# Sorted experts of a recurrent block on Trainium2: inner rows computed turned from fp16 halves, biases as a product, halves made by GpSimd in the narrow attention

## The chip, the cores and the metric

One core of one Trainium2 chip runs the whole program: four attention-like layers and four expert layers over 4096 tokens of 128 features. The metric is the device time of one execution in microseconds, the median of the runs shown. Less is better.

## The reference, cut to what matters

Three of the steps matter here. Layer 1 has an attention of 16 heads of 8 features, and then a mixture of 8 experts of which each token takes 2 (8192 rows to compute). Layer 2 has a mixture of the same shape, of which each token takes 2 too but with room for 5120 rows in all. An expert is

```
h = gelu(x @ W1[e] + b1[e])        # x 128 features, W1 128 x 512
y = h @ W2[e] + b2[e]              # W2 512 x 128
out = sum over the chosen experts of share * y
```

All inputs and outputs are fp32. The experts' biases are part of what is computed.

## The kernel before, in words

The program is a row of stages with a barrier of all engines behind each. Every engine's order of work is written out by hand; engines meet by semaphores alone.

**Narrow attention** (`narrow_attention_stage`, from L623) has 16 items of 4 heads, each with 32 steps in which TensorE computes scores (L798), row maxima of the item ahead (L784) and the weighted sum (L814), ScalarE the exponentials (L848) and VectorE the maxima (L865). Beside it GpSimd runs `RowScatter.run` (L1730): 64 indirect DMAs (L1745) that send the tokens' rows to the place where their expert's rows lie together, 4 in each item, each held back by a count of scores. SyncE loads the weights of one expert in each of items 0, 1, 3, 5, ... (`load_expert`, L1721) and clears one eighth of a table of results in items 2, 4, ... .

**Sorted experts** (`sorted_experts_stage`, from L1822) runs twice: `experts1` over 72 blocks of 128 rows (it also holds the output projection of the attention, after block 11), `experts2` over 40. A block belongs to one expert, whose number lies in a table. For a block n the engines do:

- TensorE: `turn_x` turns x of block n + 2 (L1927); `project` reads the expert's number into a register (`expert_of`, L1916) and makes rows of the inner layer in one fp32 product of 512 columns, with the tokens as the stationary operand (L1934); `turn_h` turns h of block n in four fp32 products (L1941); `down` reads the expert's number once more and sums four fp32 products (L1950).
- VectorE: `add_bias` (L2011) adds b1, kept in all 128 partitions, and `finish` (L2016) adds b2. Each reads the expert's number too.
- ScalarE: Gelu (L1990), a copy of the turned x (L1983) and of the turned h (L1996).
- GpSimd: `keep` (L1896) copies the row's target and share, `send` multiplies by the share (L1901), waits for its own result, and starts the indirect DMA of 128 rows (L1904).
- SyncE: loads x of a block ahead (L1883, L1890).

The tiles with two buffers (x turned, `up`, h, `out`) let TensorE be one block ahead of ScalarE in `project` and one behind in `down`. Most of the blocks run in a hardware loop that holds four of them; all addresses of weights are made of the expert's register at run time.

**Combine and send** (`combine_and_send_stage`, from L2530) stands between the two and loads all weights of the second experts at once (L1683 to L1685).

Of the kernel before, what the change touches and what calls it, by code (L numbers as in the profile page):

```python
# [9 lines left out]
ALU = mybir.AluOpType  # L10
# [614 lines left out]
def narrow_attention_stage(nc, ident, q_d, k_d, v_d, o_d, l_d, max_d, beside):  # L625
# [28 lines left out]
    with Stage(nc, "attn1") as st:  # L654
# [32 lines left out]
        def _(sp):  # L687
# [60 lines left out]
            body(0, 0, True, False, lambda: job.load_expert(sp, LOOPS))  # L748
            with sp.Fori(0, LOOPS) as j:
                body(2 * j + 1, 1, False, False, lambda: job.load_expert(sp, j))  # L750
                body(2 * j + 2, 0, False, False, lambda: job.clear(sp, j))
            body(NI - 1, 1, False, True, lambda: job.clear(sp, LOOPS))
# [915 lines left out]

class ExpertWeights:

    LOADS = 3

    def __init__(self, ctx, nc, name, weights_d):
        self.weights_d = weights_d
        E, _, F = weights_d[0].shape
        sb = lambda n, width: ctx.enter_context(nc.sbuf_tensor(f"{name}_{n}", [P, width], F32))
        self.w1, self.b1, self.w2 = (sb(n, E * F) for n in ("w1", "b1", "w2"))

    def load(self, sp, loaded):  # L1680

        w1_d, b1_d, w2_d, _ = self.weights_d
        sp.dma_start(self.w1[:].rearrange("d (e f) -> d e f", e=w1_d.shape[0]), w1_d.rearrange("e d f -> d e f")).then_inc(loaded, DMA)  # L1683
        sp.dma_start(self.b1[:], broadcast_rows(b1_d.rearrange("e f -> (e f)"))).then_inc(loaded, DMA)
        sp.dma_start(self.w2[:].rearrange("p (k d) -> p k d", d=D), w2_d.rearrange("e (k p) d -> p (e k) d", p=P)).then_inc(loaded, DMA)  # L1685

    def load_one(self, sp, e, loaded):

        w1_d, b1_d, w2_d, _ = self.weights_d
        F = w1_d.shape[2]  # L1690
        own = bass.ds(e * F, F)
        sp.dma_start(self.w1[:, own], w1_d[bass.ds(e, 1)].rearrange("a d f -> d (a f)")).then_inc(loaded, DMA)
        sp.dma_start(self.b1[:, own], broadcast_rows(b1_d.rearrange("e f -> (e f)")[own])).then_inc(loaded, DMA)
        sp.dma_start(self.w2[:, own].rearrange("p (k d) -> p k d", d=D),
                     w2_d[bass.ds(e, 1)].rearrange("a (k p) d -> p (a k) d", p=P)).then_inc(loaded, DMA)

class RowScatter:

    def __init__(self, st, held, send_d, share_d, xs_d, weights, blank_d=None):
        self.held, self.send_d, self.share_d, self.xs_d, self.weights, self.blank_d = held, send_d, share_d, xs_d, weights, blank_d
        self.share = st.sb("share", [P, 2, NT])
        self.send = st.sb("send", [P, 2, NT], I32)
        self.rows = st.sb("sent_rows", [P, NT, ROW])
        self.loaded, self.sent, self.weights_in = st.sem("send_loaded"), st.sem("sent"), st.sem("weights_in")
        self.copied, self.numbered = st.sem("rows_copied"), st.sem("numbered")
        if blank_d is not None:
            self.blank, self.blank_made, self.blanked = st.sb("blank", [P, BLANK * D]), st.sem("blank_made"), st.sem("blanked")
            self.experts, self.clears = weights.weights_d[0].shape[0], blank_d.shape[0] // (P * BLANK)  # L1710
# [5 lines left out]
    def load_weights(self, sp):  # L1716
        self.weights.load(sp, self.weights_in)

    def load_expert(self, sp, e):
        self.weights.load_one(sp, e, self.weights_in)  # L1720
# [9 lines left out]
    def run(self, pool, nc, hold=None):  # L1730

        if self.blank_d is not None:
            nc.gpsimd.memset(self.blank[:], 0.0).then_inc(self.blank_made, 1)
        pool.wait_ge(self.loaded, 2 * DMA)
        pool.wait_ge(self.copied, 1)
        for j in range(2):
# [11 lines left out]
        if self.blank_d is None:  # L1748
            pool.wait_ge(self.weights_in, self.weights.LOADS * DMA)
        else:  # L1750
            pool.wait_ge(self.weights_in, self.weights.LOADS * DMA * self.experts)
            pool.wait_ge(self.blanked, DMA * self.clears)
# [69 lines left out]
def sorted_experts_stage(nc, name, ident, blocks, xs_d, expert_d, weights, y_d, beside=None):  # L1822
# [4 lines left out]
    E = 8  # L1827
    F = 4 * D
    FT = F // P
    UNROLL = 4  # L1830
    NL = blocks // UNROLL
    assert blocks % UNROLL == 0 and NL >= 3
    with Stage(nc, name) as st:
        x, y = st.sb("x", [P, UNROLL, ROW]), st.sb("y", [P, blocks, D])
        result = st.sb("result", [P, blocks, 2], I32)
        w1, b1, w2 = weights.w1, weights.b1, weights.w2
        b2 = st.sb("b2", [P, E * D])
        expert = st.sb("expert", [1, blocks], I32)
        xT = st.sb("xT", [P, 2, P])
        pre, hid = st.sb("pre", [P, 2, F]), st.sb("hid", [P, 2, F])  # L1840
        hidT = st.sb("hidT", [P, 2, F])
        xt = st.ps("xt", [P, 2, CH])
        up = st.ps("up", [P, 2, F])
        ht = st.ps("ht", [P, 2, F])
        out = st.ps("out", [P, 2, CH])
        names = ("consts", "x_turned", "x_copied", "projected", "biased", "gelu_done", "h_turned", "h_copied", "summed", "y_ready")
        (consts, x_turned, x_copied, projected, biased, gelu_done, h_turned, h_copied, summed, y_ready) = (st.sem(n) for n in names)
        stored, kept, shared, loaded = st.sem("stored"), st.sem("kept"), st.sem("shared"), [st.sem(f"loaded{u}") for u in range(UNROLL)]
        job = beside(st) if beside else None
        block = st.block()  # L1850
        NCONST = 2

# [18 lines left out]
        def _(sp):  # L1871
            sp.dma_start(expert[:], expert_d[:]).then_inc(consts, DMA)
            sp.dma_start(b2[:], broadcast_rows(weights.weights_d[3].rearrange("e d -> (e d)"))).then_inc(consts, DMA)
# [19 lines left out]
        def _(pool):  # L1893
# [12 lines left out]

            for n in range(blocks + UNROLL - 1):
# [11 lines left out]
        def _(pe):  # L1919
            mm = nc.tensor.matmul  # L1920

            def turn_x(n, u, any_before):

                pe.wait_ge(loaded[u], DMA * ((n - u) // UNROLL + 1))
                if any_before:
                    pe.wait_ge(x_copied, n - 1)
# [1622 lines left out]
```

## Time and profile before

| what | us |
|---|---|
| median of 3 runs (3450.25 to 3453.23) | 3452.64 |
| profiled execution: span from first to last instruction, the only time given for it | 3455.0 |
| narrow attention, 1925 to 2567 | 642 |
| sorted experts 1, 2567 to 2798 | 231 |
| combine and send, 2798 to 2979 | 181 |
| sorted experts 2, 2979 to 3104 | 125 |

### The profile page before, as it was taken

Reading aid. Unit: us, or ns where it says so; the run is one execution under the profiler, and the core shown is the slowest. Engines: PE = TensorE matmul, PEld = TensorE weight load, DVE = VectorE, ACT = ScalarE, POOL = GpSimd, SP = SyncE. Lnnn points to the kernel's source line nnn. Section 1 sums busy time; section 2 is a strip of 40 time slices with the busy share of each in tenths; the row PEclk is TensorE's granted clock in tenths of the full one; section 3 lists DMA queues with packets and bytes.
Section 4 is the critical chain, followed back from the end, with each engine's and each line's share of the span. In section 5 each row is a group of like instructions: output and inputs, shape, how many; then the busy total and the mean of one; then the engine's idle time right before and its main releaser. Section 6 shows DMA issues by size and latency. Waiting matters only on the chain. (4 is left out here: it accounts for less than half of the span.)

```text
span 3455.0 us, 66767 instructions
## 1 busy us (share of the span) xinstructions
PE 2862.4 (83%) x21143; PEld 1283.2 (37%) x21144; DVE 2338.1 (68%) x3360; ACT 1849.0 (54%) x3005; POOL 1552.6 (45%) x1224
## 2 busy tenths in 40 slices
PE   3999999999999996799965599999978932484994
PEld 1333333333333334633323122222226622352772
DVE  5666666666666663788886799999944348534663
ACT  2555555555555551154463399999973443244442
POOL 0898999899989996200000011110115625460000
PEclk9999999999999997899986699999999965696995
DMA  2111111111111113500003222222221151113001
GB/s 86 31 42 47 43 52 46 42 48 42 56 42 48 42 48 119 197 1 1 0 2 126 66 49 56 54 53 53 53 85 47 46 182 42 29 39 100 11 13 55
DMA packets 263894, 189.55 MB, mean 55 GB/s; under 512 B 148174, under 2 KB 209990, under 8 KB 262576
## 3 DMA queue, kind: packets, MB, share of 16 engines
q1 hardware_dynamic: 255568, 174.05, 17.6%
q0 software_dynamic: 8224, 14.24, 1.3%
q8 instruction: 51, 0.84, 0.1%
q14 instruction: 51, 0.42, 0.0%
HBM read 105.21 MB, written 67.55 MB: 50 GB/s over the span
## 5 line engine op out<-in xcount | busy, mean ns | idle before, releaser
L331 POOL TENSOR_TENSOR attn_esum<-attn_esum,attn_prob 128x1024 f32<-128x1024 f32 x384 | 904.7, 2356 | 30.3 <-ACT attn_prob L482 6.7
L553 DVE TENSOR_REDUCE attn_half_max<-attn_peek 128x2 f32<-128x1024 f32 x512 | 627.0, 1225 | 398.7 <-PE attn_peek L382 394.9
L482 ACT ACTIVATE attn_prob<-attn_score 128x1024 f32<-128x1024 f32 x512 | 512.5, 1021 | 247.4 <-PE attn_score L365 247.4
L848 ACT ACTIVATE attn_prob<-attn_score 128x512 f32<-128x512 f32 x1024 | 556.3, 596 | 73.2 <-PE attn_score L798 59.0
L865 DVE TENSOR_REDUCE attn_half_max<-attn_peek 128x2 f32<-128x1024 f32 x512 | 583.5, 1214 | 11.5 <-PE attn_peek L784 11.4
L412 PE MATMUL attn_acc<-attn_prob,attn_v 128*64 128x512 f32 x2048 | 487.9, 597 | 0.1
L814 PE MATMUL attn_acc<-attn_prob,attn_v 128*32 128x256 f32 x4096 | 328.2, 392 | 12.1 <-ACT attn_out L840 10.6
L1745 POOL DMA_INDIRECT sorted_x<-attn_sent_rows,attn_send x64 | 62.5, 976 | 556.0 <-PE attn_score L798 521.1
L784 PE MATMUL attn_peek<-attn_ke,attn_qe 48*128 48x512 bf16 x1024 | 203.0, 393 | 46.1 <-DMA attn_ke<-k 31.6
L382 PE MATMUL attn_peek<-attn_hi 64*128 64x512 f16 x1024 | 200.2, 388 | 34.3 <-DVE attn_half_max L553 34.3
L331 POOL TENSOR_TENSOR attn_esum<-attn_prob 128x1024 f32<-128x1024 f32 x64 | 151.6, 2369 | 127.0 <-ACT attn_prob L482 127.0
L798 PE MATMUL attn_score<-attn_qe,attn_ke 49*128 49x512 bf16 x1024 | 200.7, 389 | 8.3 <-ACT attn_prob L848 6.0
L412 PEld LDWEIGHTS attn_acc<-attn_prob,attn_v 128*64 128x64 f32 x2048 | 130.8, 137 | 201.1 <-issue 156.4
L1539 PE MATMUL experts_up<-experts_x,experts_up_w 128*128 (+1 forms) x816 | 200.6, 382 | 4.5 <-POOL experts_sel L1517 4.5
L2011 DVE TENSOR_TENSOR experts_pre<-experts_up,experts_b 128x512 f32<-128x512 f32 x112 | 77.4, 691 | 175.5 <-PE experts_up L1934 175.0
L367 PE MATMUL attn_score<-attn_hi 64*128 64x512 f16 x1024 | 194.8, 377 | 0.0
L367 PE MATMUL attn_score<-attn_lo,attn_hi 64*128 64x512 f16 x1024 | 194.7, 377 | 0.0
L367 PE MATMUL attn_score<-attn_hi,attn_lo 64*128 64x512 f16 x1024 | 194.7, 377 | 0.0
L365 PE MATMUL attn_score<-attn_shift,attn_sel 64*128 64x512 bf16 x1024 | 194.7, 377 | 0.0
L2123 POOL MEMSET proj_zero<- 128x2340 f32 x1 | 2.1, 2052 | 376.6 <-POOLq L41 376.6
L1609 ACT ACTIVATE experts_a<-experts_up 128x512 f32<-128x512 f32 x136 | 81.2, 597 | 159.8 <-PE experts_up L1539 158.3
L1904 POOL DMA_INDIRECT picked<-experts_y,experts_result x112 | 115.7, 1033 | 87.9 <-POOL experts_y L1901 85.3
(532 smaller groups left out, 4576.0 us busy)
## 6 DMA issues: line engine op xcount, KB each, us to landing
attn_xb<-attn_x_all SPq DMA_DIRECT2D x66, 256.0 KB
attn_invB<-inv SPq DMA_DIRECT2D x64, 256.0 KB
o<-attn_out SPq DMA_DIRECT2D x32, 512.0 KB
out_o<-o SPq DMA_DIRECT2D x8, 2048.0 KB
mix_f<-picked SPq DMA_DIRECT2D x16, 512.0 KB, 7.3
experts_x<-sorted_x SPq DMA_DIRECT2D x112, 65.0 KB
attn_qe<-q SPq DMA_DIRECT2D x192, 32.0 KB
attn_ke<-k SPq DMA_DIRECT2D x192, 32.0 KB
```

Of the source, the lines that this page charges most:

```text
L331: nc.gpsimd.tensor_tensor(own, before, prob[:, u % NPROB, :, :], ALU.add).then_inc(added, 1)
L367: last = mm(score[:, u % 2, h, :], ks[r, slot, WHICH["k"], keys], qs[r, slot, WHICH["q"], queries], start=(n == 0), stop=False)
L382: last = mm(peek[:, h, :], hi[r, slot, WHICH["q"], t * P:(t + 1) * P], hi[r, slot, WHICH["k"], half * CH:(half + 1) * CH], start=True, sto ...
L412: last = mm(acc[rows_of(h), :], v[:, slot, t, rows_of(h)], prob[:, u % NPROB, h, :], start=(t == 0), stop=(t == KT - 1))
L482: nc.scalar.activation(prob[:, u % NPROB, :, :], score[:, u % 2, :, :], ACT.Exp).then_inc(exped, 1)
L553: V.tensor_reduce(half_max[:, half, :, t], peek[:], AX.X, ALU.max, negate=True).then_inc(maxed, 1)
L784: last = mm(peek[:, m % NPEEK, n, :], qe[r, slot, pair, t * P:(t + 1) * P], ke[r, slot, pair, half * CH:(half + 1) * CH], start=True, stop ...
L798: last = mm(score[:, (PAIR * k + n) % RING, :], ke[r, slot, pair, t * P:(t + 1) * P], qe[r, slot, pair, c * CH:(c + 1) * CH], start=True, ...
L814: last = mm(acc[h * COL:(h + 1) * COL, cols], v[:, slot, t, h, :], prob[:, (HG * s + h) % NPROB, cols], start=(t == 0 and p == 0), stop=(t ...
L848: nc.scalar.activation(prob[:, n % NPROB, :], score[:, n % RING, :], ACT.Exp).then_inc(exped, 1)
L865: V.tensor_reduce(half_max[:, half, PAIR * pair:PAIR * (pair + 1), t], peek[:, m % NPEEK, :, :], AX.X, ALU.max, negate=True).then_inc(maxe ...
L1539: ins = nc.tensor.matmul(out, ws[pw][:, cols], xs[px][own], start=start and n == 0, stop=stop and n == 2)
```

## The change

Weights, x and h become a sum of two fp16 numbers (a high half, and a low half that is the rest), and each product becomes three (high by high, high by low, low by high). Scales of 16 and 128 keep the halves in range. In detail:

- `project` computes h turned: for each of four slices of 128 inner features the weights are the stationary operand and the turned tokens are the moving one; three products of 128 columns, and a fourth of the bias' halves by a constant tile `unit`. With h turned already, `turn_h`, its PSUM tile and its copy fall away; ScalarE's third step now makes the high half of h.
- `down` has three products a slice, and a thirteenth for b2.
- VectorE makes the low halves of x and of h, and multiplies the result by the share (`finish`); `add_bias` and its register loads are gone. GpSimd's `send` loses the multiplication and the wait for it.
- In the narrow attention SyncE now loads an expert's weights in each of the 16 items, alternating between layer 1 and layer 2, into one of two raw tiles, and waits before it for GpSimd to have split what the raw tile held. GpSimd splits a unit after every fourth send and one after the last. Halves of layer 1 stay in SBUF; those of layer 2 go to memory by a DMA of GpSimd's and are loaded by the combine stage, which also clears the biases' tile.

The core of the diff, with lines of the loop bodies only:

```diff
             def project(n, s, any_before):
                 e = expert_of(pe, n)
-                pe.wait_ge(x_copied, n + 1)
+                pe.wait_ge(x_split, n + 1)
                 if any_before:
-                    pe.wait_ge(biased, n - 1)
-                mm(up[:, s, :], xT[:, s, :], w1[:, bass.ds(e * F, F)], start=True, stop=True).then_inc(projected, 1)
-
-            def turn_h(n, s, any_before):
-                pe.wait_ge(gelu_done, n + 1)
-                if any_before:
-                    pe.wait_ge(h_copied, n - 1)
+                    pe.wait_ge(gelu_done, n - 1)
                 for k in range(FT):
-                    last = nc.tensor.transpose(ht[:, s, k * P:(k + 1) * P], hid[:, s, k * P:(k + 1) * P], ident[:])
-                last.then_inc(h_turned, 1)
+                    own = up[:, s, k * P:(k + 1) * P]
+                    for m, (pw, px) in enumerate(PARTS):
+                        mm(own, w1[:, pw, bass.ds(e * F + k * P, P)], xT[px][:, s, :], start=(m == 0), stop=False)
+                    last = mm(own, bias[:, bass.ds(e * PER + k * P, P)], unit[:], start=False, stop=True)
+                last.then_inc(projected, 1)
 
             def down(n, s, any_before):
                 e = expert_of(pe, n)
-                pe.wait_ge(h_copied, n + 1)
+                pe.wait_ge(h_split, n + 1)
                 if any_before:
                     pe.wait_ge(y_ready, n - 1)
                 for k in range(FT):
-                    last = mm(out[:, s, 0:D], hidT[:, s, k * P:(k + 1) * P], w2[:, bass.ds(e * F + k * D, D)], start=(k == 0), stop=(k == FT - 1))
-                last.then_inc(summed, 1)
+                    for m, (pw, ph) in enumerate(PARTS):
+                        mm(out[:, s, 0:D], hT[ph][:, s, k * P:(k + 1) * P], w2[:, pw, bass.ds(e * F + k * D, D)],
+                           start=(k == 0 and m == 0), stop=False)
+                mm(out[:, s, 0:D], unit[:], bias[:, bass.ds(e * PER + F, D)], start=False, stop=True).then_inc(summed, 1)
...
+            def rest_of_h(n, s):
+                dve.wait_ge(h_high, n + 1)
+                V.scalar_tensor_tensor(out=hT[1][:, s, :], in0=hid[:, s, :], scalar=H_SCALE, in1=hT[0][:, s, :],
+                                       op0=ALU.mult, op1=ALU.subtract).then_inc(h_split, 1)
...
             def send(n):
                 pool.wait_ge(kept, n + 1)
                 pool.wait_ge(y_ready, n + 1)
-                nc.gpsimd.tensor_scalar(y[:, n, :], y[:, n, :], result[:, n, 1:2].bitcast(F32), None, ALU.mult).then_inc(shared, 1)
-                pool.wait_ge(shared, n + 1)
...
+    def halves(self, nc, link, raw, high, low):
+
+        link(nc.gpsimd.tensor_scalar(raw, raw, ExpertSource.W_SCALE, 0.0, ALU.mult, ALU.add))
+        link(nc.gpsimd.tensor_copy(high, raw))
+        return nc.gpsimd.tensor_tensor(low, raw, high, ALU.subtract)
...
             for t in range(NT):
-                if hold:
-                    hold(j * NT + t)
+                n = j * NT + t
+                hold(n)
...
+                if n and n % self.SENDS == 0:
+                    self.split_unit(pool, nc, link, n // self.SENDS - 1)
             pool.wait_ge(self.sent, (j + 1) * NT * DMA)
...
+        self.split_unit(pool, nc, link, 2 * self.experts - 1)
```

How the program's order on TensorE reads in the hardware loop of `experts2`: ISA is a register operation done by the sequencer (the trace calls it FUSED_REGOPS), `experts_w` the weights, `experts_up` the rows of the inner layer, `experts_out` those of the result. The middle of `project` and the start of `turn_h`, before:

```order
L1934 ISA [waits norm0_dve_step,norm0_loaded2]
L1934 MATMUL experts_up<-experts_w,experts_xT 128x512
L1939 REGISTER_ALU [waits norm0_var_ready]
L1941 MATMUL experts_ht<-identity,experts_hid 128x128 [waits norm0_xn_ready]
L1941 MATMUL experts_ht<-identity,experts_hid 128x128 x3
```

And now the first of four slices of `project`, which stand one behind the other:

```order
L1997 ISA [waits norm0_std_ready,norm0_dve_step]
L1997 MATMUL experts_up<-experts_xT,experts_w 128x128 x2
L1997 ISA
L1997 MATMUL experts_up<-experts_xT,experts_w 128x128
L1998 ISA
L1998 MATMUL experts_up<-experts_unit,experts_bias 128x128
```

One register operation and one product became twelve operations and sixteen products; the wait and the four products of `turn_h` are gone. In `down`, before:

```order
L1950 ISA [waits norm0_evacuated]
L1950 MATMUL experts_out<-experts_w,experts_hidT 128x128
L1950 ISA
L1950 MATMUL experts_out<-experts_w,experts_hidT 128x128
L1950 ISA
```

And now, the start and the end:

```order
L2008 ISA [waits attn0_maxed]
L2008 MATMUL experts_out<-experts_w,experts_hT 128x128 x2
L2008 ISA
L2008 MATMUL experts_out<-experts_w,experts_hT 128x128
L2008 ISA
```
```order
L2008 MATMUL experts_out<-experts_w,experts_hT 128x128
L2010 ISA
L2010 MATMUL experts_out<-experts_bias,experts_unit 128x128
```

Four register operations and four products became nine and thirteen. The two reads of the expert's number (an ISA, a TENSOR_LOAD and two ISA each) stand where they stood.

## Rows read from the trace of the kernel before

**Rows 1.** Windows of the narrow attention, experts 1, combine and experts 2.
```profile
core 0: us, PE busy (x) PEld busy (x) DVE busy (x) ACT busy (x) POOL busy (x), PEclk, DMA share, GB/s
1925.00:2567.00 642.00, 594.82 (x6144) 168.17 (x6144) 594.11 (x577) 568.14 (x1056) 63.35 (x68) 0.97 0.22 50
2567.00:2798.00 231.00, 197.78 (x1144) 140.28 (x1144) 84.26 (x162) 94.48 (x217) 131.67 (x216) 0.97 0.22 63
2979.00:3104.00 125.00, 105.46 (x600) 73.01 (x600) 39.29 (x80) 52.92 (x121) 72.92 (x120) 0.95 0.17 46
```
**Rows 2.** Lines L1927 and L1904, window 2640:2784: 51 blocks (duration min/median/max, first and last start).
```profile
L1927 PE MATMUL experts_xt<-identity,experts_x x51: 272/273/273, 2641.3 to 2781.9; 128*128 128x128 f32 x51
L1904 POOL DMA_INDIRECT picked<-experts_y,experts_result x51: 1025/1040/1049, 2640.8 to 2781.5; - x51
```
**Rows 3.** Six lines of TensorE's sequencer over one block of experts 1, windows within 2703.6:2706.5.
```profile
L1931 PEldq ALU_OP  x2: 32/32/32, 2703.7 to 2706.4; - x2
L1934 PEldq FUSED_REGOPS  x1: 46/46/46, 2703.9 to 2703.9; - x1
L1939 PEldq ALU_OP  x1: 32/32/32, 2704.0 to 2704.0; - x1
L1916 PEldq FUSED_REGOPS  x2: 42/96/151, 2704.1 to 2704.6; - x2
L1916 PEldq TENSOR_LOAD <-experts_expert x1: 361/361/361, 2704.2 to 2704.2; - x1
L1916 PEldq SEQ_ASSERT  x1: 18/18/18, 2704.8 to 2704.8; - x1
L1948 PEldq ALU_OP  x1: 32/32/32, 2704.9 to 2704.9; - x1
L1926 PEldq EVENT_SEMAPHORE  x1: 51/51/51, 2705.5 to 2705.5; - x1
L1916 PEldq FUSED_REGOPS  x2: 42/96/151, 2705.6 to 2706.1; - x2
L1916 PEldq SEQ_ASSERT  x1: 18/18/18, 2706.3 to 2706.3; - x1
```
**Rows 4.** Line L1950, windows 2704.98:2705.40 and 2705.15:2705.39.
```profile
L1950 PEldq FUSED_REGOPS  x4: 46/46/46, 2705.0 to 2705.4; - x4
L1950 PEldq FUSED_REGOPS  x2: 46/46/46, 2705.1 to 2705.3; - x2
```
**Rows 5.** Line L1904, window 2600:2618: GpSimd catching up after a stall.
```profile
L1904 POOL DMA_INDIRECT picked<-experts_y,experts_result x6: 1025/1032/1040, 2602.3 to 2615.2; - x6
```
**Rows 6.** Timeline (start, us) of one block of experts 1.
```profile
2640.75 1.04 POOL L1904 DMA_INDIRECT picked<-experts_y,experts_result  x1 [0.77 <-POOL experts_y L1901]
2641.11 0.62 ACT L1990 ACTIVATE experts_hid<-experts_pre 128x512 f32<-128x512 f32 x1
2641.63 0.27 ACT L1983 ACTIVATE experts_xT<-experts_xt 128x128 f32<-128x128 f32 x1
2641.80 0.19 POOL L1896 COPY experts_result<-experts_x 128x2 int32<-128x2 int32 x1
2642.12 0.60 POOL L1901 TENSOR_SCALAR experts_y<-experts_y,experts_result 128x128 f32<-128x128 f32 x1
```
**Rows 7.** Timeline and windows (granted clock ahead of DMA share): eight bf16 products at two clocks.
```profile
1420.73 0.65 PE L1078 MATMUL out_trb<-out_ident,out_parts 128*96 128x128 bf16 x8 [1.27 <-DVE out_cT L1202]
1422.54 1.09 PE L1078 MATMUL out_trb<-out_ident,out_parts 128*96 128x128 bf16 x8 [1.17 <-DVE out_cT L1202]
...
1420.70:1421.40 0.70, 0.65 (x8) 0.50 (x8) 0.63 (x3) 0.00 (x0) 0.00 (x0) 1.00 0.72 187
1422.50:1423.40 0.90, 0.86 (x8) 0.86 (x9) 0.82 (x3) 0.00 (x0) 0.00 (x0) 0.50 1.00 303
```
**Rows 8.** Lines elsewhere that do what the change adds to VectorE and ScalarE.
```profile
L1644 DVE SCALAR_TENSOR_TENSOR experts_h<-experts_h x136: 679/680/693, 1461.8 to 1771.5; 128x512 f16<-128x512 f32 x136
L1636 DVE SCALAR_TENSOR_TENSOR experts_up_w<-experts_up,experts_up_w x10: 278/690/692, 1442.8 to 1448.9; 128x512 f16<-128x512 f32 x8, 128x128 f16<-128x128 f32 x2
L1596 ACT ACTIVATE experts_h<-experts_h x136: 619/621/630, 1459.7 to 1770.9; 128x512 f16<-128x512 f32 x136
```
**Rows 9.** Waits in the narrow attention; GpSimd elementwise lines; VectorE's maxima in both attentions.
```profile
POOL sorted_x L1745 <- PE attn_score L798: 521.1, 63, 17.2
L331 POOL TENSOR_TENSOR attn_esum<-attn_esum,attn_prob x384: 2332/2354/2384, 91.4 to 1322.3; 128x1024 f32<-128x1024 f32 x192
L553 DVE TENSOR_REDUCE attn_half_max<-attn_peek x512: 1207/1226/1228, 62.7 to 1291.1; 128x2 f32<-128x1024 f32 x171
L865 DVE TENSOR_REDUCE attn_half_max<-attn_peek x512: 1182/1214/1228, 1932.0 to 2534.0; 128x2 f32<-128x1024 f32 x171
```
**Rows 10.** Timeline: end of the narrow attention, first work of experts 1, its x-wait.
```profile
2554.27 0.97 POOL L1745 DMA_INDIRECT sorted_x<-attn_sent_rows,attn_send  x1 [5.53 <-PE attn_score L798]
2564.24 1.13 SPq L721 DMA_DIRECT2D sums<-attn_out  x4
2567.36 0.22 SPq L1872 DMA_DIRECT2D experts_expert<-owner  x1
...
2595.05 0.33 PE L1927 MATMUL experts_xt<-identity,experts_x 128*128 128x128 f32 x1 [2.99 <-DMA experts_x<-sorted_x]
```

More of the change, by code:

```diff
@@ L1698, with __init__ @@
 class RowScatter:
-    def __init__(self, st, held, send_d, share_d, xs_d, weights, blank_d=None):
+    SENDS = 4
+    def __init__(self, st, held, send_d, share_d, xs_d, weights, later, blank_d):
         self.held, self.send_d, self.share_d, self.xs_d, self.weights, self.blank_d = held, send_d, share_d, xs_d, weights, blank_d
+        self.sources = (weights.source, later)
+        E, F, PER = later.E, later.F, later.PER
+        self.experts = E
         self.share = st.sb("share", [P, 2, NT])
@@ L1705, in __init__ @@
         self.rows = st.sb("sent_rows", [P, NT, ROW])
[L1706 to L1710, printed above, removed]
+        self.loaded, self.sent, self.copied, self.numbered = (st.sem(n) for n in ("send_loaded", "sent", "rows_copied", "numbered"))
+        self.blank, self.blank_made, self.blanked = st.sb("blank", [P, BLANK * D]), st.sem("blank_made"), st.sem("blanked")
+        self.clears = blank_d.shape[0] // (P * BLANK)
+        self.raw, self.parts = st.sb("raw_w", [P, 2, 2, F]), st.sb("w_parts", [P, 2, 2, F], F16)
+        self.raw_bias, self.bias_parts = st.sb("raw_bias", [E, 2, PER]), st.sb("bias_parts", [E, 2, 2, PER], F16)
+        self.raw_in, self.step, self.split, self.parts_out, self.bias_in, self.bias_out, self.bias_kept = (
+            st.sem(n) for n in ("raw_in", "split_step", "split", "parts_out", "bias_in", "bias_out", "bias_kept"))
     def load(self, sp):
@@ L1714, in load, with load_expert @@
         sp.dma_start(self.share[:], self.share_d[:]).then_inc(self.loaded, DMA)
[L1716 to L1720, printed above, removed]
+        for layer, source in enumerate(self.sources):
+            _, b1_d, _, b2_d = source.weights_d
+            sp.dma_start(self.raw_bias[:, layer, 0:source.F], b1_d).then_inc(self.bias_in, DMA)
+            sp.dma_start(self.raw_bias[:, layer, source.F:source.PER], b2_d).then_inc(self.bias_in, DMA)
+    def load_expert(self, sp, layer, e, unit, slot):
+        if not (isinstance(unit, int) and unit == 0):
+            sp.wait_ge(self.split, unit)
+        self.sources[layer].load_one(sp, e, self.raw[:, slot, :, :], self.raw_in)
     def clear(self, sp, n):
@@ L1746, in run @@
                                         bounds_check=self.xs_d.shape[0] - 1, oob_is_err=False).then_inc(self.sent, DMA)
+                if n and n % self.SENDS == 0:
+                    self.split_unit(pool, nc, link, n // self.SENDS - 1)
             pool.wait_ge(self.sent, (j + 1) * NT * DMA)
[L1748 to L1752, printed above, removed]
+        self.split_unit(pool, nc, link, 2 * self.experts - 1)
+        pool.wait_ge(self.split, 2 * self.experts + 1)
+        pool.wait_ge(self.parts_out, DMA * self.experts)
+        pool.wait_ge(self.bias_kept, DMA)
+        pool.wait_ge(self.blanked, DMA * self.clears)
 class DividedProjection:
@@ L1822, in sorted_experts_stage @@
 def sorted_experts_stage(nc, name, ident, blocks, xs_d, expert_d, weights, y_d, beside=None):
-    E = 8
-    F = 4 * D
+    E, F, PER = weights.source.E, weights.source.F, weights.source.PER
     FT = F // P
+    X_SCALE, W_SCALE, H_SCALE = ExpertSource.X_SCALE, ExpertSource.W_SCALE, ExpertSource.H_SCALE
+    PARTS = ((0, 0), (0, 1), (1, 0))
     UNROLL = 4
     NL = blocks // UNROLL
-    assert blocks % UNROLL == 0 and NL >= 3
+    assert blocks % UNROLL == 0 and NL >= 3 and X_SCALE == H_SCALE
     with Stage(nc, name) as st:
@@ L1958, in body @@
                     project(n + 1, 1 - s, not (first and u == 0))
-                turn_h(n, s, not (first and u < 2))
                 if not (first and u == 0):
                     down(n - 1, 1 - s, not (first and u < 3))
-            pe.wait_ge(consts, NCONST * DMA)
+            pe.wait_ge(consts, DMA)
+            pe.wait_ge(unit_step, 2)
             turn_x(0, 0, False)
```

169 lines of the change are left out of this document (104 added, 65 removed).

## The prediction

> **What bounds the kernel now.** I read the windows by stage first. The change touches four stages, and of their 1179 us the two sorted-expert stages take 231 and 125 [rows 1]. In them no engine is full: TensorE shows 198 of 231 us busy, and since its products overlap in the record that is more than it works. So I looked for the pace. In the steady part 50 blocks pass in 140.6 us, 2.81 us each, on TensorE and on GpSimd alike [rows 2]. GpSimd can go faster: after a stall it starts five further sends in 12.9 us, 2.58 each [rows 5]. ScalarE works 0.62 + 0.27 + 0.60 us in a block [rows 6]. None of these sets 2.81.
>
> The sequencer of TensorE does. Over one block its own instructions stand in a row without a hole [rows 3]: 2703.7 (arithmetic for the wait of `project`), 2703.9 (address of W1), 2704.0 (wait of `turn_h`), 2704.1 to 2704.8 (the expert's number: two register operations, a load of 0.30 to 0.36 us, an assertion), 2704.9 (wait of `down`), 2705.0 to 2705.4 (four addresses of W2), 2705.5 (wait of `turn_x`), 2705.6 to 2706.3 (the number again), 2706.4 (the next block's arithmetic). That is 2.7 us, and the loop's branch, once in four blocks, makes the rest of the 2.81. Matmuls are handed over in between and run later from the queue. The reader should see that the duration of a register operation, 46 ns, isn't its price: four of them, each with one fp32 product, fit in a window of 0.42 us, and the fourth starts behind 2705.39, so a step is 0.11 to 0.14 us [rows 4]. Without a product between, 2704.1 to 2704.2, it is 0.1 [rows 3].
>
> **The change part by part.**
>
> *TensorE's register operations.* `project` goes from 1 to 12 and `down` from 4 to 9, as the order of the program shows: 16 more in a block. Each stands alone in front of one or two products. An fp32 product is recorded as two weight loads and two matmuls, so an operation with two fp16 products hands over as much as the 0.13 us step does; one with a single product less. Bounds for a step: 0.10 (nothing between) and 0.14. I take 0.12, nearer to the rows with a product. 16 x 0.12 = 1.92 us.
>
> *What TensorE's sequencer loses:* the wait of `turn_h` with its four products, 2704.0 to 2704.1 [rows 3], 0.1 us by the rounded rows; I take 0.13. The two reads of the number, 0.8 us each, stay. Net +1.79 us a block, 2.81 to 4.60. Over 112 blocks +200 us. With 0.10 it is 1.47 and +165. With 0.14, and 0.03 for a second product behind each of 8 operations, it is 2.35 and +263; the rounded rows make that a loose end, since 0.14 would need all three steps at the window's edge, and I set the upper bound at 0.13: 2.19 and +245.
>
> *TensorE's array.* Eight bf16 products of 128 columns with their own weights took 0.65 us from first start to last end at granted clock 1.00 [rows 7]. One takes 0.22 us, so the pitch is (0.65 - 0.22) / 7 = 0.06 us, and 29 in a block take 1.8 us with the turn of x. At granted clock 0.50 the same eight took 1.09 us, a pitch of (1.09 - 0.34) / 7 = 0.107, 29 of them 3.1 us. Busy for under half of a block, TensorE may be granted the lower of its levels (2.4 and 1.2 GHz): the fast stages show 0.95 to 0.97 [rows 1] at 86% busy. Either way the array stays under 4.60 us, and its queue holds what it lags. I cost it at nothing; if the register operations were free it would be the cover that is gone.
>
> The Trainium skill (TensorE: Matmul & The Clock Gate, Back-to-back issue gap) gives about 81 ns for a weight load with its 128-column product where these rows give 60. By it, as an estimate, the 29 products would take 2.35 us, still under the sequencer's 4.60.
>
> *VectorE, ScalarE, GpSimd.* VectorE now does 0.28 for x, 0.68 for h [rows 8] and about 0.3 for the result, 1.3 us, and loses its reads of the number. ScalarE keeps three steps of 0.62, 0.27 and 0.62 [rows 6, 8]. GpSimd loses 0.60 and most of a wait of 0.77 [rows 6]: from 2.58 to 1.2 to 1.8. All are covered by TensorE's 4.60. New waits: VectorE's `finish` waits for GpSimd's `keep`, which needs only x; TensorE's `down` waits for the low half of h, finished some 2 us after `project` of that block, while a whole block of TensorE's order lies between. So they cost nothing while the pace is 4.60.
>
> *Stalls that go.* Early in experts 1 TensorE waited 2.99 us for x once [rows 10] and a little at neighbours; slower blocks give the loads time: -5. At the end of each stage GpSimd sends without the multiplication: -1.4 twice, say -3.
>
> *Narrow attention.* GpSimd waited 521 of 642 us for its turn [rows 9]. A unit is three passes over 128 x 1024: the subtraction like the 2.35 us addition [rows 9]; the scaling between 1 and 4.8 us (8 times the 0.60 of 128 columns [rows 6]); the cast between the same. So 5 to 12 us, 16 units 80 to 190 us, inside the 521. SyncE's new wait for unit i - 2, split at the start of item i - 1, is met a whole item (about 38 us) earlier; behind it in SyncE's order stand the store and the shift of the next item, for which everything waits, so the cover matters, but it is three times the unit. VectorE's maxima took 1.226 us where GpSimd was adding all the time and 1.214 here [rows 9]: at most 0.012 x 512 = 6 us, by GpSimd's fifth of the time 1 us. The last unit comes after the last send at 2554.27 and its landing: some 2.5 us, 5 to 12 for the unit, about 3 for the DMA out, hence ready at 2566 to 2573 against 2567.3 now [rows 10]: 0 to +6, I take +2. Extra loads and stores of 0.5 MB per item meet a DMA share of 0.22 [rows 1].
>
> The Trainium skill (GPSIMD Engine Reference, Specifications) warns that GpSimd shares its SBUF interfaces with VectorE instructions that have two SBUF inputs or a 2-port mode. VectorE's maxima have one input, from PSUM, and the pair of rows just named shows under 1%.
>
> *Combine.* A clear of 5120 fp16 and one load instead of three, both ahead of need: 0.
>
> **Sum:** 3455.0 + 200 - 5 - 3 + 3 = 3650 against the profiled execution, whose span is 2.4 us over the median of 3452.64. So 3648 us. Low end 3455 + 165 - 12 = 3608, high end 3455 + 245 + 6 = 3706.
>
> **The rivals.**
> 1. *The other side: register operations are prepared while products are handed over, and don't add up.* Then the sequencer keeps two reads of 0.8 and three waits of 0.1, about 2.0 us; array 1.8, GpSimd up to 1.8: 2.1 us a block, -0.7 x 112 = -79 and -6: 3370. It decides where a step costs under 0.01 us, for then the 16 added ones (0.13) only repay the lost wait of `turn_h`. For it speaks that a product handed over behind an operation costs only 0.03 (0.13 against 0.10), so that much of the hand-over does run beside the sequencer. Against it speak rows 3 and 4, in which each operation takes its 0.1.
> 2. *The array at the lower clock is the bound, register operations being free:* 3.2 us a block, +0.4 x 112 - 6: 3493. Against it the same rows.
> 3. *An operation costs only its recorded 46 ns:* 16 x 0.046 - 0.13 = +0.6, x 112 = +68: 3515.
> 4. *The sequencer and more:* at the lower clock the array lags, results come late and TensorE's waits stop being met; or a slow GpSimd delays the shift in the attention. 0.5 us a block or 3 us an item, +50: 3700 to 3760.
>
> The skill's 81 ns rule, if the array alone were the bound, would give an estimate of 2.46 us a block and about 3410; it shares rival 1's condition and is counted there.
>
> **How the numbers follow.** Forecast 0.80, rival 1 0.08 (with 0.02 of it ending near no change), rival 2 0.04, rival 3 0.03, rival 4 0.05. The predicted time is 3648. The forecast's own bounds are 3608 to 3706; widened a little to both sides, 3595 to 3715, it holds the forecast and part of rival 4, 0.82. A measurement of this kernel can tell 0.2%, 7 us, from no change. Faster 0.06, same 0.02, slower 0.92.
>
> **What would show it.** Right: blocks of 4.5 to 4.7 us in both stages; TensorE's sequencer without holes, 21 operations of 46 ns a block at steps near 0.12 us; GpSimd idle most of the block before each send; a lower granted clock in the expert stages; the narrow attention at 642 us within 5. Wrong: steps under 0.06 us between register operations; waits of TensorE on `x_split` or `h_split`; ScalarE or VectorE without gaps; an attention that grew by more than 10 us. What would undo the prediction is chiefly that the register operations with products between them are cheaper than the four of `down`.

## The result, and the profile after

| | before | after |
|---|---|---|
| median, us | 3452.86 (3450.25 to 3453.23, 4 runs) | 3672.80 (3665.89 to 3679.33, 4 runs) |
| profiled execution: its time | 3455.0 (span) | 3665.89, span 3664.2 |
| ratio of the medians | | 1.0638, 95% interval 1.0623 to 1.0653 |
| mean granted clock | 0.917 | 0.876 |

The change costs 220 us by the medians and 209.2 by the spans of the two profiled executions (the one of after was the fastest of its four). By the first and last instructions of the stages the 209.2 are: experts 1 +125.7, experts 2 +67.2, the narrow attention with what lies between its last store and the experts' first load +20.2, combine -0.5, and all that stands before the attention -3.4. The last is scatter between executions, since nothing was changed there: the attention starts at 1913.3 in this trace and at 1915.5 to 1917.5 in those of the six variants of the changed kernel below.

The windows by stage of the changed kernel, columns as in [rows 1], for the narrow attention, experts 1 and experts 2:

```profile
1922.00:2584.00 662.00, 594.42 (x6144) 168.43 (x6144) 610.55 (x577) 568.13 (x1056) 145.13 (x130) 0.97 0.23 58
2584.00:2943.00 359.00, 263.79 (x2224) 212.27 (x2224) 106.09 (x234) 101.50 (x217) 99.16 (x146) 0.66 0.13 39
3121.00:3315.00 194.00, 139.77 (x1200) 110.38 (x1200) 52.15 (x120) 56.95 (x121) 53.61 (x82) 0.68 0.10 27
```

In the expert stages every engine became idler than in [rows 1], TensorE too (74% of 359 us where it was 86% of 231), and its granted clock fell to a mix of its two levels. In the attention GpSimd works 82 us more, and the window is 20 us longer.

The pace of the blocks, answering to [rows 2], is read from the turn of x in both stages and from GpSimd's send:

```profile
L1987 PE MATMUL experts_xt<-identity,experts_x x57: 279/421/472, 2660.3 to 2925.5; 128*128 128x128 f32 x57
L1987 PE MATMUL experts_xt<-identity,experts_x x34: 280/419/469, 3141.5 to 3297.9; 128*128 128x128 f32 x34
L1961 POOL DMA_INDIRECT picked<-experts_y,experts_result x58: 980/1170/1463, 2662.0 to 2931.3; - x58
```

(2925.5 - 2660.3) / 56 = 4.74 us, and (3297.9 - 3141.5) / 33 = 4.74 as well. TensorE's sequencer over one block, answering to [rows 3] and [rows 4] (PEldq lines, window 2700.8 to 2705.6):

```profile
L1976 PEldq TENSOR_LOAD <-experts_expert x3: 300/302/312, 2700.8 to 2705.4; - x3
L2005 PEldq EVENT_SEMAPHORE  x1: 51/51/51, 2701.5 to 2701.5; - x1
L2008 PEldq FUSED_REGOPS  x8: 46/46/60, 2701.6 to 2702.5; - x8
L2010 PEldq FUSED_REGOPS  x1: 60/60/60, 2702.6 to 2702.6; - x1
L1984 PEldq FUSED_REGOPS  x1: 97/97/97, 2702.8 to 2702.8; - x1
L1986 PEldq EVENT_SEMAPHORE  x1: 51/51/51, 2702.9 to 2702.9; - x1
L1993 PEldq EVENT_SEMAPHORE  x1: 51/51/51, 2703.8 to 2703.8; - x1
L1997 PEldq FUSED_REGOPS  x8: 46/46/51, 2703.9 to 2705.2; - x8
L1998 PEldq FUSED_REGOPS  x4: 46/46/46, 2704.1 to 2705.3; - x4
```

The row has no hole: number of `down` read (2700.8), wait (2701.5), nine addresses (2701.6 to 2702.6), arithmetic and wait of `turn_x` (2702.8, 2702.9), number of `project`, wait (2703.8), twelve addresses (2703.9 to 2705.3), number of `down` again (2705.4). Twelve operations recorded at 46 to 51 ns start within 1.4 us: (2705.3 - 2703.9) / 11 = 0.127 us a step, whether one or two fp16 products stand behind an operation.

In the attention the waits and the maxima answer to [rows 9]:

```profile
POOL sorted_x L1806 <- PE attn_score L802: 459.7, 56, 17.2
ACT attn_prob L852 <- PE attn_score L802: 74.4, 53, 37.2
L869 DVE TENSOR_REDUCE attn_half_max<-attn_peek x512: 1183/1214/1228, 1928.7 to 2545.2; 128x2 f32<-128x1024 f32 x171
L875 DVE TENSOR_TENSOR attn_nmax<-attn_half_max x32: 174/176/1404, 1946.9 to 2546.4; 128x16 bf16<-128x16 f32 x32
```

GpSimd still spends 459.7 us waiting for scores (521.1 before), so it isn't short of time. ScalarE waits 74.4 us for scores, where it was 59.0. The maxima themselves are as short as before (1214 ns), yet the 512 of them now span 616.5 us, where they spanned 602.0 [rows 9]. The last row is the merge of the maxima. In the kernel before the same line read:

```profile
L871 DVE TENSOR_TENSOR attn_nmax<-attn_half_max x32: 174/175/177, 1950.2 to 2535.3; 128x16 bf16<-128x16 f32 x32
```

Its longest went from 177 to 1404 ns. It is not one outlier: 15 of the 32 merges take 1.27 to 1.40 us, one for each of the 15 splits that stand among the sends, and the other 17 take 174 to 176 ns. One such case in the timeline of after, VectorE and GpSimd:

```profile
2003.79 1.31 DVE L875 TENSOR_TENSOR attn_nmax<-attn_half_max 128x16 bf16<-128x16 f32 x1
2005.25 0.21 DVE L880 STREAM_TRANSPOSE attn_nmaxT<-attn_nmax 128x32 bf16<-128x32 bf16 x1
...
2003.01 0.97 POOL L1806 DMA_INDIRECT sorted_x<-attn_sent_rows,attn_send  x1 [16.86 <-PE attn_score L802]
2004.00 1.06 POOL L1755 TENSOR_SCALAR attn_raw_w<-attn_raw_w 128x1024 f32<-128x1024 f32 x1
2005.13 1.04 POOL L1756 CAST experts_w<-attn_raw_w 128x1024 f16<-128x1024 f32 x1
2006.25 2.13 POOL L1757 TENSOR_TENSOR experts_w<-attn_raw_w,experts_w 128x1024 f16<-128x1024 f32 x1
```

The merge stands from 2003.79 to 2005.10. At its usual 0.175 us it would have ended just before GpSimd's scaling starts (2004.00); it ends with the scaling instead (2005.06). A unit's three passes take 1.06 + 1.04 + 2.13 = 4.2 us. The sends that a unit follows wait for the ninth score of an item, and the merge belongs to that same step, so the two meet in item after item. A send alone doesn't lengthen the merge: in the kernel before it runs beside one as well (a send from 2006.97 to 2007.95, a merge of 0.176 us at 2007.75).

The end of the attention, answering to [rows 10]:

```profile
2573.43 0.80 POOL L1778 DMA_DIRECT2D expert_w<-attn_w_parts  x1 [0.30 <-POOL attn_w_parts L1757]
...
2576.44 1.14 SPq L721 DMA_DIRECT2D sums<-attn_out  x4
2584.13 0.23 SPq L1932 DMA_DIRECT2D experts_expert<-owner  x1
```

From the last store (2576.44 + 1.14) to the first load of the experts 6.5 us pass, where it was 2567.36 - 2564.24 - 1.13 = 2.0 [rows 10]. What fills the gap is a DRAIN in the sequencer of GpSimd (POOLq), with which it goes to the barrier of all engines. After, and before:

```profile
L39 POOLq DRAIN  x1: 6193/6193/6193, 2577.1 to 2577.1; - x1
```
```profile
L39 POOLq DRAIN  x1: 5284/5284/5284, 2556.7 to 2556.7; - x1
```

It takes 5.3 us in the kernel before too, but there it ends at 2562.0, ahead of the last stores. Now it starts only when GpSimd's own last transfer has landed (a wait up to 2576.9), and ends at 2583.3; the first load of the experts follows at 2584.1. So the 20.2 us are 14.5 of maxima, 4.5 of this gap, and 1 between the last maximum and the last store.

### The profile page after: what moved, and what is told of

Same layout as the page of the kernel before. It is cut to its first block and busy times, and to the rows that moved or that the text cites. A ratio compares the mean times of both kernels' runs of the same rounds, so it can differ in the third digit from the quotient of the medians.

```text
span 3664.2 us, 71084 instructions
## 1 busy us (share of the span) xinstructions
PE 2957.4 (81%) x22823; PEld 1389.6 (38%) x22824; DVE 2389.7 (65%) x3471; ACT 1860.2 (51%) x3005; POOL 1591.2 (43%) x1180
## 5 line engine op out<-in xcount | busy, mean ns | idle before, releaser
L852 ACT ACTIVATE attn_prob<-attn_score 128x512 f32<-128x512 f32 x1024 | 556.3, 596 | 88.7 <-PE attn_score L802 74.4
L869 DVE TENSOR_REDUCE attn_half_max<-attn_peek 128x2 f32<-128x1024 f32 x512 | 583.3, 1214 | 10.3 <-PE attn_peek L788 10.3
L1961 POOL DMA_INDIRECT picked<-experts_y,experts_result x112 | 130.0, 1161 | 390.0 <-DVE experts_y L2079 381.7
L1806 POOL DMA_INDIRECT sorted_x<-attn_sent_rows,attn_send x64 | 63.3, 989 | 486.8 <-PE attn_score L802 459.7
L2079 DVE TENSOR_SCALAR experts_y<-experts_out,experts_result 128x128 f32 (+1 forms) x112 | 39.2, 350 | 330.3 <-PE experts_out L2010 330.3
L1997 PE MATMUL experts_up<-experts_xT,experts_w 128*128 128x128 f16 x1344 | 183.9, 279 | 61.8 <-issue 40.0
L2008 PE MATMUL experts_out<-experts_w,experts_hT 128*128 x1344 | 152.8, 288 | 63.5 <-issue 63.0
```

Source lines behind the costliest of these rows:

```text
L852: nc.scalar.activation(prob[:, n % NPROB, :], score[:, n % RING, :], ACT.Exp).then_inc(exped, 1)
L869: V.tensor_reduce(half_max[:, half, PAIR * pair:PAIR * (pair + 1), t], peek[:, m % NPEEK, :, :], AX.X, ALU.max, negate=True).then_inc(maxe ...
```

## The experiments

Two theories stood for the expert stages: the sequencer's register operations set 4.74 us, or the products (29, at a lower clock) and the waits between engines do. For the attention: VectorE's merge stands still while GpSimd splits, or SyncE's extra loads and GpSimd's work at large lengthen an item. The ratios are to the kernel before, run on the same chip; its median there was 3454.4 for `a_static`, `a_bias`, `a_keep` and `a_shift`. A difference "against after" is to the 3672.8 above, beside which the kernel before read 3452.9, so it is good to about 2 us.

**Constant addresses** (`a_static`).
```
-  mm(own, w1[:, pw, bass.ds(e * F + k * P, P)], ...)      # and w2, bias likewise
+  mm(own, w1[:, pw, k * P:(k + 1) * P], ...)
```

> The changed kernel, but the 21 addresses of weights and biases on TensorE are constants (every block uses the weights of expert 0, so the output is another); the expert's number is still read twice a block, and products, shapes, waits and transfers stay. If the sequencer's register operations set the 4.74 us of a block at 0.125 us each, 21 x 0.125 = 2.6 us go from it; then the sequencer keeps about 2.1 us and the array (1.8 us at granted clock 1.00, 3.1 at 0.50) comes next: blocks of 2.1 to 3.2 us, so 170 to 290 us less in 112 blocks, 3380 to 3500 us. If the 29 products at the lower clock, or the waits between engines, set the block, nothing changes: 3673 within 7.

Every block now uses the weights of expert 0, so the result is another and this is no repair. Measured 3401.6 us (ratio 0.984, 0.983 to 0.986): -271 against after. The turn of x and the window 2660 to 2770 of this kernel:

```profile
L1987 PE MATMUL experts_xt<-identity,experts_x x49: 278/279/283, 2660.2 to 2765.5; 128*128 128x128 f32 x49
...
2660.00:2770.00 110.00, 97.77 (x1520) 87.80 (x1516) 63.34 (x151) 70.32 (x151) 64.56 (x101) 1.00 0.20 57
```

Blocks of (2765.5 - 2660.2) / 48 = 2.19 us with every product still there, so the 21 operations had cost (4.74 - 2.19) / 21 = 0.121 us each. The sequencer's own row has no hole here either: the two reads of the number and the waits fill it, so no other bound cuts this price short. The clock is 1.00 here and 0.66 in after: it is low where TensorE idles behind its sequencer. The theory of products and waits falls.

**Constant addresses of the biases alone** (`a_bias`).
```
-  last = mm(own, bias[:, bass.ds(e * PER + k * P, P)], unit[:], ...)
+  last = mm(own, bias[:, k * P:(k + 1) * P], unit[:], ...)     # and F:F + D for b2
```

> The changed kernel, but the five addresses of the bias products of a block are constants (biases of expert 0 throughout, so the output is another); the products themselves stay. Sequencer: five operations of 0.125 us less, 4.74 to 4.11 us a block, -70 us, 3603. If the price lies in the products that are handed over and not in the operations: 0, 3673 within 7. If an operation costs only its 46 ns: -26 us.

Measured 3597.4 us (1.041, 1.040 to 1.043): -75, five operations at 75.5 / 112 / 5 = 0.135 us. By the operation's recorded 46 ns it would have been 26. The turn of x:

```profile
L1987 PE MATMUL experts_xt<-identity,experts_x x55: 280/305/472, 2661.1 to 2880.5; 128*128 128x128 f32 x55
```

(2880.5 - 2661.1) / 54 = 4.06 us a block, the same 0.135 for each of the five.

**The number read once** (`a_keep`).
```
 def down(n, s, any_before, u):
-    e = expert_of(pe, n)
+    e = number_again(u)      # pe.snap(held[u]) for u in (0, 3), else the value that project read
```
`project` copies its number into `held[u]` for u = 0 and 3, so that it survives the loop's edge.

> The changed kernel, but TensorE reads a block's number once: down takes it from a register kept since project two blocks earlier (across the loop's edge by two copies in four blocks). Result unchanged. Sequencer: a read of about 0.8 us a block goes and half a register operation comes, 4.74 to 4.0 us, -75 to -90 us, 3583 to 3598. If the reads run beside the array's backlog and cost nothing: 0.

Measured 3603.0 us (1.042, 1.041 to 1.044): -70, 5 us short of the least expected. Its blocks:

```profile
L1998 PE MATMUL experts_xt<-identity,experts_x x27: 299/323/448, 2660.2 to 2767.0; 128*128 128x128 f32 x27
```

(2767.0 - 2660.2) / 26 = 4.11 us, -0.63 for one read less and half an operation more. A read is worth 0.7 us, not 0.8.

**More operations for the same columns** (`b_slices`, on the kernel before).
```
-  mm(up[:, s, :], xT[:, s, :], w1[:, bass.ds(e * F, F)], ...)
+  for k in range(FT):
+      last = mm(up[:, s, k * P:(k + 1) * P], xT[:, s, :], w1[:, bass.ds(e * F + k * P, P)], ...)
```

> The kernel before, with project's one product of 512 columns cut into four of 128 at four register addresses: three more register operations a block, the same fp32 columns for the array, result unchanged. Sequencer: +3 x 0.125 = +0.375 us a block, +42 us, 3495. If the array or GpSimd (2.58 us) sets the block: 0 to +10 us (three more short weight loads).

Measured 3488.1 us (1.010, 1.009 to 1.012; before 3452.5): +36. The turn of x:

```profile
L1927 PE MATMUL experts_xt<-identity,experts_x x35: 272/273/327, 2660.6 to 2769.4; 128*128 128x128 f32 x35
```

(2769.4 - 2660.6) / 34 = 3.20 us, +0.39 for three operations. The 36 us are less than 0.39 x 112 = 44: the two expert stages grew by 20.4 and 12.7 us, so their first blocks and ends didn't pay the full price.

**The split one send later** (`a_shift`).
```
-  if n and n % self.SENDS == 0:
+  if n > 1 and n % self.SENDS == 1:
```

> The changed kernel with each of GpSimd's splits in the narrow attention moved one send later (behind sends 5, 9, ..., 61 in place of 4, 8, ..., 60), so that it no longer starts when VectorE merges its maxima. If the merge (1.31 us where it was 0.175) costs the 1.14 us of each item because GpSimd works on the same memory at that moment: items back at 37.6 us, -15 to -17 us, 3657. If the items are longer for SyncE's loads or for GpSimd's work anywhere in the item: 0 to -3 us.

Measured 3654.0 us (1.057, 1.056 to 1.059): -19, somewhat more than the 15 to 17 expected. Merge and maxima:

```profile
L869 DVE TENSOR_REDUCE attn_half_max<-attn_peek x512: 1181/1216/1228, 1931.0 to 2531.8; 128x2 f32<-128x1024 f32 x171
L875 DVE TENSOR_TENSOR attn_nmax<-attn_half_max x32: 174/174/177, 1949.2 to 2533.0; 128x16 bf16<-128x16 f32 x32
```

The same splits and loads, and the maxima span 600.8 us. The loads and GpSimd's work as such cost nothing that shows; where the split stands does. From the attention's first load to that of the experts this kernel takes 653.7 us, against 670.8 in after and 650.6 before; what is left is less than the 4.5 of the gap at the end, which stayed.

**The merge with one operand** (`a_merge`, the split where the change put it).
```
-  V.tensor_tensor(nmax..., half_max[:, 0, :, tiles], half_max[:, 1, :, tiles], ALU.min)
+  V.tensor_reduce(nmax..., half_max[:, :, :, tiles].rearrange("p a h t -> p h t a"), AX.X, ALU.min)
```

> The changed kernel, its splits where they were, but VectorE's merge of the two halves of the maxima is a reduction over one operand in SBUF in place of an operation on two; result unchanged. If two operands in SBUF are what makes VectorE stand while GpSimd works: the merge is at 0.18 to 0.35 us in every item, items back to about 37.6 us, -15 to -19 us, 3654 to 3658. If any VectorE work on SBUF stands while GpSimd works: the merge or the transpose behind it still reaches 1.3 us in half of the cases, 0 to -3 us, 3670 to 3673.

Measured 3657.3 us (1.058, 1.055 to 1.060; before 3453.8): -16.

```profile
L869 DVE TENSOR_REDUCE attn_half_max<-attn_peek x512: 1182/1217/1227, 1930.9 to 2532.2; 128x2 f32<-128x1024 f32 x171
L875 DVE TENSOR_REDUCE attn_nmax<-attn_half_max x32: 186/188/190, 1949.1 to 2533.5; 128x16 bf16<-128x32 f32 x32
L880 DVE STREAM_TRANSPOSE attn_nmaxT<-attn_nmax x32: 211/212/213, 1949.3 to 2533.7; 128x32 bf16<-128x32 bf16 x32
```

With the same 32 numbers of each partition read as one operand the merge never stands, though GpSimd's scaling starts at the same send. One such case:

```profile
2006.36 0.19 DVE L875 TENSOR_REDUCE attn_nmax<-attn_half_max 128x16 bf16<-128x32 f32 x1
...
2006.57 1.06 POOL L1755 TENSOR_SCALAR attn_raw_w<-attn_raw_w 128x1024 f32<-128x1024 f32 x1
```

It stands 0.21 us ahead of the scaling, as the merge of two operands did (2003.79 and 2004.00). So it is the form with two operands in SBUF that waits; the one with a single operand has just ended when the scaling starts, so what it would cost in the midst of one isn't shown, and the kind of operation changed together with the number of operands. By the same stretch the attention takes 658.3 us here, 12.5 less than in after; the traces of `a_static`, `a_bias` and `a_keep`, which leave the attention alone, give 670.9 to 674.6, so one trace is good to some 4 us.

**What stands behind the sequencer in the kernel before** (`b_dve`, `b_keep`, `b_both`, `b_all`). `b_keep` is the edit of `a_keep`, made on the kernel before. `b_dve`:
```
-  nc.gpsimd.tensor_scalar(y[:, n, :], y[:, n, :], result[:, n, 1:2].bitcast(F32), None, ALU.mult).then_inc(shared, 1)
+  V.tensor_scalar(own, own, share, None, ALU.mult).then_inc(y_ready, 1)      # in finish, behind the bias
```

> The kernel before, with the multiplication by the share moved from GpSimd to VectorE, behind its addition of the bias; result unchanged. GpSimd loses 0.60 us and a wait of 0.77 a block. Sequencer of TensorE at 2.81: no change, or -1 to -3 us at the stages' ends, 3451 within 5. If GpSimd's 2.58 us were the bound with something on top: -0.3 us a block or more, -30 us or more.

> The kernel before, but TensorE reads a block's number once and down takes it from a register kept since project (two copies in four blocks); result unchanged. Sequencer: 2.81 to 2.15 us, then GpSimd's 2.58 us is the next bound: -0.23 x 112 = -26 us, 3428. If GpSimd already bounds: 0. If nothing stands behind the sequencer before 2.15: -70 us.

> The kernel before with both edits, the kept number and the multiplication on VectorE; result unchanged. Neither bound is left at 2.5: the sequencer at about 2.15, VectorE with its two reads of the number and three steps at 2.2 to 2.5: blocks of 2.2 to 2.5 us, -35 to -65 us, 3388 to 3418. If the two edits were only additive in the small gains of each (one alone 0, the other -26): 3428.

> The kernel before with the number kept on TensorE, the multiplication on VectorE, and the number kept on VectorE too; result unchanged. With the first two alone VectorE read the number twice in each block of 2.4 to 2.5 us and stood between the product and the Gelu. If VectorE's sequencer is now the bound: its 0.65 us a block goes and another 0.1 us is lost elsewhere, blocks of 2.1 to 2.2 us, -20 to -40 us against those two alone, 3385 to 3405. If the loop through project, bias, Gelu, turn and down is a matter of latency and not of VectorE's sequencer: 0 to -10 us, 3415 to 3426.

| kernel | median, us | ratio (95%) | block, us |
|---|---|---|---|
| `b_dve` | 3451.2 | 0.9995 (0.9986 to 1.0005) | 2.84 |
| `b_keep` | 3432.3 | 0.994 (0.992 to 0.996) | 2.54 |
| `b_both` | 3425.6 | 0.992 (0.990 to 0.993) | 2.58 |
| `b_all` | 3428.1 | 0.991 (0.989 to 0.993) | 2.56 |

(Before 3452.5 for the first three and 3456.0 for the last; blocks from the turns of x between 2660 and 2770.) GpSimd without its multiplication changes nothing, the sequencer without one read does. The turns of x of `b_keep`, `b_both` and `b_all`:

```profile
L1938 PE MATMUL experts_xt<-identity,experts_x x42: 272/273/273, 2661.9 to 2766.0; 128*128 128x128 f32 x42
```
```profile
L1936 PE MATMUL experts_xt<-identity,experts_x x43: 272/273/273, 2661.1 to 2769.5; 128*128 128x128 f32 x43
```
```profile
L1936 PE MATMUL experts_xt<-identity,experts_x x43: 272/273/273, 2660.2 to 2767.9; 128*128 128x128 f32 x43
```

The further edits gain nothing over `b_keep` in these blocks (the 7 us that `b_both` is faster by lie in the rest of the two stages), though `b_both` was expected at 2.2 to 2.5 and `b_all` 20 to 40 us below it. Neither GpSimd nor VectorE's sequencer is what stands next. The windows 2640 to 2770 of the kernel before and of `b_all`:

```profile
2640.00:2770.00 130.00, 118.37 (x697) 83.41 (x696) 45.49 (x93) 58.95 (x138) 83.84 (x138) 1.00 0.17 45
```
```profile
2640.00:2770.00 130.00, 124.97 (x763) 91.17 (x764) 64.26 (x153) 69.79 (x153) 59.22 (x103) 1.00 0.18 49
```

TensorE is busy 96% of the time at full clock, against 91%. That its fp32 products now fill it is the likely reading; it wasn't isolated, and the other theory in the expectation of `b_all`, the latency of the chain through bias, Gelu, turn and `down`, isn't excluded.

**The changed kernel repaired** (`a_all`): `a_shift`, `a_keep`, and
```
+  sp.wait_ge(self.split, 2 * self.experts + 1)
+  sp.dma_start(self.sources[1].parts_d[:, :, :, ...], self.parts[:]).then_inc(self.last_out, DMA)
```

> The changed kernel with the split one send later, TensorE's number kept, and the last unit of halves stored by SyncE in place of GpSimd; result unchanged. If the effects add: -19 for the split, -70 for the number, and the attention's last store comes closer to the start of the experts (6.5 us apart after the change, 2.0 before): -2 to -5 us; 3579 within 6. If the 6.2 us that GpSimd spends before the barrier doesn't hang on its own last transfer: only the first two, 3584, and the gap stays 6.5 us.

Measured 3580.3 us (1.036, 1.034 to 1.037). The effects add. The end of its attention:

```profile
2559.48 0.60 SPq L1756 DMA_DIRECT2D expert_w<-attn_w_parts  x1
...
2562.51 1.14 SPq L721 DMA_DIRECT2D sums<-attn_out  x4
2566.66 0.23 SPq L1940 DMA_DIRECT2D experts_expert<-owner  x1
```

3.0 us between last store and first load instead of 6.5 (`a_shift` alone kept 6.6). GpSimd still sets the barrier, only sooner:

```profile
L39 POOLq DRAIN  x1: 6112/6112/6112, 2559.7 to 2559.7; - x1
```

With no transfer of its own to wait for, its DRAIN starts 17.4 us earlier than in after and ends at 2565.8, where SyncE was ready at 2564.8: some 1 us is still its doing, which is the difference to the 2.0 of the kernel before. The whole attention, from its first load to that of the experts, takes 650.9 us, as in the kernel before (650.6), with all 16 splits in it. `b_keep`, `b_both` and `b_all` beat both kernels; no form of the changed one that computes the same result does.

## Why the prediction held, step by step

The forecast was 3648 within 3595 to 3715, slower with 0.92; 3672.8 came. The direction, the mechanism of the expert stages and the range held; the median lies 25 us above the forecast. By the spans it is 14 (3664.2 against 3650): the attention is 17 too long, and the scatter ahead of it and combine take 4 off. The other 11 come from which executions were profiled: the one of before ran 2 us over its median, the one of after 9 us under it. The sum's low end takes off 12 us where its terms name 8, and the measured blocks of 4.74 us lie just past the 4.5 to 4.7 named as the sign of being right; nothing hangs on either.

**What bounds: right.** No other engine, no clock and no transfer but TensorE's sequencer set both paces. `a_static`, `a_bias` and `b_slices` price a register operation at 0.121, 0.135 and 0.129 us.

**Sixteen steps at 0.12: mis-sized by little.** 16 x 0.127 = 2.03, less 0.1 for `turn_h`'s wait, is the +1.93 a block that the rows show; 1.79 had been summed. x 112 that is 216 and not 200. The step lies inside the bounds, nearer to 0.13, and no surcharge for a second fp16 product behind an operation shows. The 0.1 for the wait of `turn_h` is what its rounded rows said and what makes the sum fit; it wasn't measured by itself.

**Stalls and ends at -8: too little.** The stages grew by 125.7 and 67.2, in sum 192.9, where 1.93 x 112 gives 216. So -23 came from first blocks and ends. Of it the 2.99 us wait for x is gone, as forecast, but an earlier one of 0.74 us is now 1.96; the rest wasn't taken apart. This error and the one of the step cancel, and that is luck: 192.9 against the predicted 192.

**The array at nothing: right.** `a_static` computes all 29 products and a turn in a block of 2.19 us at clock 1.00, which fits the 1.8 us worked out from [rows 7]. The 81 ns of the Trainium skill (TensorE: Matmul & The Clock Gate, Back-to-back issue gap) would need 29 x 0.081 = 2.35 us, as an estimate from that page; this trace doesn't agree, since the whole block is shorter.

**"Narrow attention at 642 within 5": wrong, and this is the step that failed.** It grew by 20.2 us, past the 10 that the prediction had named as a sign of being wrong; the number survived because the expert stages carry nine tenths of the change. The prediction looked for harm to VectorE's maxima, which read PSUM alone, found under 1%, and set aside the rule of the Trainium skill (GPSIMD Engine Reference, Specifications) that GpSimd shares its SBUF interfaces with VectorE instructions that have two SBUF inputs. It didn't ask which *other* VectorE instruction of the stage has two. One of 0.175 us does, and it stood 1.31 us under GpSimd's scaling, right in the step that the sends were tied to. Here the trace agrees with that rule: 15 merges stand, the maxima end 14.5 us late, and `a_merge` and `a_shift` bring 16 to 19 us back (12.5 and 17.1 in the attention itself). The cost of the unit itself, 4.2 us where 5 to 12 were bounded, was hidden as said.

**The tail at +2: too small.** The last unit's passes ended at 2573.1 and its transfer was still to come, where the forecast had all of it ready by 2566 to 2573: the whole attention was late, and with it the last send. The forecast also had no term for GpSimd's DRAIN of 5.3 to 6.2 us at the stage's end. It had been hidden behind the last stores; behind GpSimd's own transfer it was exposed, and the gap to the experts grew by 4.5 us. `a_all` gave 3.5 of it back.

**VectorE's maxima +1: zero**, their median stayed at 1214 ns.

**The rivals.** Register operations prepared beside the products (3370), at 46 ns (3515) or free with a slow array (3493) are excluded by the prices above. The fourth, sequencer and more, named a GpSimd that delays the attention; that is what came on top, though by another way than a late shift, and with 20 us instead of 50.

## What to carry to other kernels

When a product's address is made at run time, count the register operations on the engine's sequencer and price them by the distance between their starts (here 0.12 to 0.13 us), not by their recorded 46 ns: cheap products lose to them, and a wide product that needs one address can beat three quick ones that need three. Before work goes to an idle GpSimd, list the VectorE instructions with two SBUF operands that will stand beside it, the shortest too, and place it between them. A number that is read twice should be kept in a register: that one edit made the kernel before 0.6% faster.

## What was not expected of the hardware

- The granted clock followed the sequencer: 0.66 with blocks of 4.74 us, 1.00 with the same products in 2.19 us. No cost of it shows: at 0.66 the sequencer's row still has no hole.
- A VectorE instruction of 0.175 us on two SBUF operands stood until the end of a GpSimd instruction of 1.06 us, 1.31 us in all, although its recorded start lies 0.2 us ahead of GpSimd's; one that reads the same data as a single operand took 0.188 us at that place.
- GpSimd's DRAIN on its way to the barrier took 5.3 to 6.2 us in the kernel before and in four forms of the changed one. A stage's last small transfer therefore costs by who issues it: 6.5 us from the last store to the next stage where it was GpSimd's and the DRAIN came behind it, 3.0 where SyncE issued it and the DRAIN ran beside the stores.
